# Two transformer layers on one core: exponentials left in their PSUM score bank, first layers in fewer and halved steps, a new order of the work

## The reference

```
x = layernorm(x + attn0(x))   # rms norm, global latent attention (16 heads, 4 kv heads, head size 8,
                              #   rope, q and k normed, causal), then a local one with a window of 32
x = layernorm(x + moe(x))     # 8 experts, top 2, each gelu(x @ W1 + b1) @ W2 + b2
x = layernorm(x + linear(x))  # q, k = elu(.) + 1, v; running sums over tokens, head size 64
x = layernorm(x + local(x))   # two layers: 8 heads of 64, shifted tokens, q and k of unit length,
                              #   rotary, softmax over a window of 64 plus the one before,
                              #   then a gated gelu feed-forward (341 hidden)
```

## Time and profile before

| | |
|---|---|
| median of 3 runs | 2406.52 us (2402.61 to 2421.29) |
| the profiled execution | 2405.99 us, span 2404.2 us |
| granted TensorE clock, mean | 0.916 of 2.4 GHz |
| busy: PE, PEld, DVE, ACT, POOL | 1938.3, 1187.6, 1168.7, 1166.9, 765.6 us |
| fillers (L537) | 1523 matmuls |

### The profile page before, as it was taken

The page is one execution under the profiler, slowest core; times in us unless marked ns, Lnnn a source line. Parts: engine busy times, 40 slices in busy tenths (PEclk is TensorE's granted clock), DMA queues, the critical chain, the costliest instruction groups (busy, mean ns, idle before and its releaser), DMA issues.

```text
span 2404.2 us, 40371 instructions
## 1 busy us (share of the span) xinstructions
PE 1938.3 (81%) x15498; PEld 1187.6 (49%) x15498; DVE 1168.7 (49%) x2324; ACT 1166.9 (49%) x2708; POOL 765.6 (32%) x654
## 2 busy tenths in 40 slices
PE   4885473689996899879989789859988799878886
PEld 2233371445444586534445567524445568545554
DVE  4124103655365534765346543665437543666564
ACT  2642041167853364257854265237774357236462
POOL 1420202065240523155331343026523143135350
PEclk8997596789998899989999899979999899989998
DMA  4000250000000252000000234000000044001010
GB/s 131 1 1 1 96 175 18 0 14 19 6 10 14 84 168 60 7 17 19 6 5 19 70 119 123 5 9 14 14 6 14 6 144 153 15 18 23 14 23 9
DMA packets 52945, 99.23 MB, mean 41 GB/s; under 512 B 11423, under 2 KB 26003, under 8 KB 52627
## 3 DMA queue, kind: packets, MB, share of 16 engines
q1 hardware_dynamic: 47059, 87.74, 12.3%
q0 software_dynamic: 4096, 8.40, 1.2%
q10 hardware_dynamic: 1600, 0.52, 0.1%
HBM read 66.02 MB, written 13.83 MB: 33 GB/s over the span
## 4 chain that ended last, share of the span: by engine, by line
PE 50%; DVE 21%; ACT 10%; POOL 8%; issue 7%; DMA 3%; SPq 1%; ACTq 0%; DVEq 0%; POOLq 0%
PE PB L537 4%; PE PH L778 4%; PE PD L537 4%; PE PB L1167 4%; PE PB L1187 3%; PE PB L1100 3%; PE PD L826 2%; PE PH L1011 2%; ACT front_arena L1298 2%; POOL x_rows L2118 2%; ACT back_arena L1446 2%; PE PD L1000 2%; PE PB L1121 2%; POOL front_arena L2096 2%; PE PB L1223 2%
## 5 line engine op out<-in xcount | busy, mean ns | idle before, releaser
L1298 ACT ACTIVATE front_arena<-PD 128x1024 f32<-128x1024 f32 (+3 forms) x384 | 297.0, 815 | 109.6 <-PE PD L826 107.8
L2156 POOL TENSOR_TENSOR back_arena<-back_arena 128x512 f32<-128x512 f32 x128 | 185.8, 1457 | 513.3 <-DVE back_arena L1961 513.1
L2096 POOL TENSOR_TENSOR front_arena<-front_arena,tri 128x256 f32<-128x256 f32 x256 | 190.9, 760 | 229.4 <-ACT front_arena L1298 228.3
L537 PE MATMUL PB<-ident 128*128 128x512 f16 x823 | 223.3, 392 | 23.1 <-DVE back_arena L1961 13.9
L1446 ACT ACTIVATE back_arena<-PB,fnm 128x128 f32<-128x128 f32 x512 | 181.1, 369 | 104.4 <-DVE fnm L1968 104.2
L1167 PE MATMUL PB<-wqkv,hT 128*128 128x512 f32 x384 | 216.1, 649 | 13.8 <-ACT hT L1416 9.2
L2161 POOL TENSOR_TENSOR fy<-fm,minus_half 128x16 f32<-128x16 f32 x64 | 187.5, 2930 | 77.4 <-DVE fm L1984 75.7
L1968 DVE TENSOR_REDUCE fnm<-PB 128x4 f32<-128x512 f32 x128 | 88.4, 691 | 246.5 <-PE PB L1187 246.2
L537 PE MATMUL PD<-ident 128*128 128x512 f16 x618 | 177.2, 408 | 9.9 <-DVE front_arena L1815 4.1
L778 PE MATMUL PH<-front_arena 128*32 128x512 f32 (+3 forms) x1536 | 164.9, 501 | 19.0 <-POOL front_arena L2096 17.2
L537 PEld LDWEIGHTS PB<-ident 128*128 128x128 f16 x823 | 78.3, 100 | 131.8 <-issue 41.5
(11 more groups left out here) (278 smaller groups left out, 3829.5 us busy)
## 6 DMA issues: line engine op xcount, KB each, us to landing
front_arena<-in_W SPq DMA_DIRECT2D x60, 514.0 KB, 4.9
W<-in_W SPq DMA_DIRECT2D x32, 514.0 KB, 3.6
back_arena<-back_arena SPq DMA_DIRECT2D x128, 128.0 KB, 2.4
y_rows<-front_arena SPq DMA_DIRECT2D x20, 256.0 KB, 5.5
front_arena<-x_rows SPq DMA_DIRECT2D x8, 512.0 KB, 4.2
out_y<-Nb SPq DMA_DIRECT2D x64, 32.0 KB, 1.6
X<-in_L_attn_hidden SPq DMA_DIRECT2D x56, 32.0 KB, 1.9
front_arena<-x_rows SPq DMA_DIRECT2D x4, 448.0 KB, 5.3
```

The costliest lines, as they stand in the source:

```text
L537: pe.matmul(bank[:, 0:512].rearrange("p (a b) -> p a b", b=128), ident16[:, :], ident16[:, :].unsqueeze(1).to_broadcast([128, 4, 128]), st ...
L1298: act.activation(pb[:, :, 0:n], p[:, :, 0:n], ACT.Exp, scale=INV_SQRT_HD).then_inc(freed(b, "S", half, g, kc, jp), 1)
L2096: pool.tensor_tensor(pb, pb, tri[:, :].unsqueeze(1).to_broadcast([128, 2, 128]), ALU.mult).then_inc(sg("masked"), 1)
L2156: pool.tensor_tensor(T1[k % 2][:, hs, :], T1[k % 2][:, hs, :], T2[:, hs, :], ALU.add).then_inc(sg("rot"), 1)
```

## The change

In the back, `exps` writes the exponentials over the scores in their own PSUM bank. The bank is freed by `softmax` on DVE, which reads it and writes the product to SBUF, and no longer by ACT. The exponentials wait no more until TensorE has turned the last tile's probabilities; `softmax` does. The order of the pieces in `back_labels` and the three banks are as before.

In the front: (1) the scaled x is written in two halves (`by_halves`), and its transposes, its copy and the first projections follow by halves, at every `toT`. (2) `rope` is 2 x 3 instructions over four tiles each. (3) The squares for the norm of q and k are taken by ACT from the projection's bank (into `QKsq`), before the rotation, and DVE's squaring is gone. (4) The rest of q is 2 instructions over all tiles, the first of which waits for the first of ACT's two only. (5) `rk` is 2 matmuls, and DVE does the running sum over tiles (4 small instructions more); `slots` and `sc` stand ahead of `GT` and `b2`. (6) One copy in the gate is gone. (7) `lq` and `lk` are one piece `lqk`, 128 rows high; ACT copies `lvt`; in `lo` the products that don't need the masked scores come first. (8) The sum of x into R ahead of the layer norm `x1` is moved up to the local attention's start.

Both tables are new: the fillers are 1298, in batch 0's front 114 where there were 242, in the merged batches' fronts 362 where there were 458, in batch 3's back 184 where there were 135. The diff, cut to its core:

```diff
-        for t in range(NT):
-            add(("rope", a, t), 0, 0.8, 0, 0.8)
+        for t in (0, 4):
+            add(("rope", a, t), 0, 1.7, 0, 1.7)
...
+    add(("slots",), 0, 5, 0, 5)
+    for t in range(NT):
+        add(("sc", t), 0, 3)
     add(("GT",), 1, 2.5, 1)
     add(("b2",), 2, 3, 0, 1.3)
-    add(("slots",), 0, 4, 0, 4)
-    for t in range(NT):
-        add(("sc", t), 0, 3)
...
-20003051610002030000000231111010032310000040000000000000000001002200000000000000000000000140000101000100032100510000ar00a200020170001074102230a0033060
...
+204000810000000010000000010002000220100000403000000000000000000022021000200000001010000101401000000300130501000000000000a00002010100102000112000400000
...
-                    pe.wait_ge(sg("src"), 5 * b + i + 1)
-                    for t in range(NT):
+                    pe.wait_ge(sg("src"), 10 * b + 2 * i + 1)
+                    for t in range(4):
+                        ins = pe.transpose(place(p, t), src[:, t, :], ident[:, :])
+                    ins.then_inc(sg("half_turned"), 1)
+                    pe.wait_ge(sg("src"), 10 * b + 2 * i + 2)
+                    for t in range(4, NT):
                         ins = pe.transpose(place(p, t), src[:, t, :], ident[:, :])
...
-                    for t in range(NT):
-                        pe.matmul(p[:, E * NT:E * NT + E], ones_m, both[:, E * t:E * t + E], start=(t == 0), stop=(t == NT - 1))
-                    pe.matmul(p[:, 0:NT * E], tri[:, :], both, start=True, stop=False, skip_group_check=True)
-                    for t in range(NT - 1):
-                        later = p[:, E * (t + 1):E * NT].rearrange("p (t e) -> p t e", e=E)
-                        ins = pe.matmul(later, ones_m, both[:, E * t:E * t + E].unsqueeze(1).to_broadcast([128, NT - 1 - t, E]),
-                                        start=False, stop=(t == NT - 2), skip_group_check=True)
-                    ins.then_inc(filled(b, "rk"), 1)
+                    pe.matmul(p[:, NT * E:2 * NT * E], ones_m, both, start=True, stop=True, skip_group_check=True)
+                    pe.matmul(p[:, 0:NT * E], tri[:, :], both, start=True, stop=True,
...
+                    def project(name, w, n):
                         p = fill(pe, b, name)
-                        is_free(pe, b, "toT", 3)
+                        pe.wait_ge(sg("half_xT"), 4 * b + 4)
                         for k in range(2):
-                            ins = pe.matmul(p[0:HL, 512 * k:512 * k + 512], lw[:, w, :],
+                            if k:
+                                is_free(pe, b, "toT", 3)
+                            ins = pe.matmul(p[0:HL * n, 512 * k:512 * k + 512], lw[:, w:w + n, :].rearrange("p a b -> p (a b)"),
...
                     p = fill(pe, b, "lo")
+                    is_free(pe, b, "lM")
+                    for t in range(NT):
+                        c = 128 * t
+                        pe.matmul(p[:, c + HL:c + HL + 1], lqz[:, c:c + 128], ones[0:HL, :],
+                                  start=(t % 4 == 0), stop=True, skip_group_check=True)
+                    for t in range(1, NT):
+                        c = 128 * t
+                        pe.matmul(p[:, c:c + HL], lqT[:, c:c + 128], lM[:, t, :], start=False, stop=False, skip_group_check=True)
                     pe.wait_ge(sg("l_A"), b + 1)
                     for t in range(NT):
-                        pe.matmul(p[:, 128 * t:128 * t + HL], lA[:, t, :], lkt[:, t, :],
...
-                    pe.wait_ge(sg("softmax"), 2 * k + 1 + r)
+                    is_free(pe, b, "fs", l, t, r)
...
-                    p = read(act, b, "toT", i)
-                    act.activation(xT[:, PAD:PAD + S], p, ACT.Copy).then_inc(freed(b, "toT", i), 1)
+                    act.wait_ge(sg("half_turned"), 4 * b + i + 1)
+                    p = slot(b, "toT", i)
+                    act.activation(xT[:, PAD:PAD + 512], p[:, 0:512], ACT.Copy).then_inc(sg("half_xT"), 1)
+                    read(act, b, "toT", i)
+                    act.activation(xT[:, PAD + 512:PAD + S], p[:, 512:S], ACT.Copy).then_inc(freed(b, "toT", i), 1)
...
-                                act.activation(QK[:, 4 * i:4 * i + 4, :], p[:, :, 0:160], ACT.Copy).then_inc(freed(b, "qkv", a, i), 1)
+                                act.activation(QK[:, 4 * i:4 * i + 4, :], p[:, :, 0:160], ACT.Copy).then_inc(sg("qk_in"), 1)
+                                act.activation(QKsq[:, 4 * i:4 * i + 4, :], p[:, :, 0:160], ACT.Square).then_inc(freed(b, "qkv", a, i), 1)
...
                     if k:
-                        read(act, *of_tile("fp", k - 1, r))
+                        act.wait_ge(sg("inverted"), 2 * k - 1 + r)
                     for h in range(4 * r, 4 * r + 4):
                         c = 128 * (h - 4 * r)
-                        ins = act.activation(fP[:, h, :], p[:, c:c + 128], ACT.Exp,
+                        ins = act.activation(p[:, c:c + 128], p[:, c:c + 128], ACT.Exp,
                                              bias=fnm[:, h:h + 1], accum_out=fden[:, h:h + 1])
-                    ins.then_inc(freed(b, "fs", l, t, r), 1)
...
+                def by_halves(dst, src):
+
+                    for h in range(2):
+                        hs = slice(4 * h, 4 * h + 4)
+                        dve.tensor_tensor(dst[:, hs, :], src[:, hs, :], st_y[:, hs].unsqueeze(2).to_broadcast([128, 4, D]),
+                                          ALU.mult).then_inc(sg("src"), 1)
+                    counts["src"] = counts.get("src", 0) + 2
+                    dve.wait_ge(sg("src"), counts["src"])
 
...
-                    for t in range(NT):
-                        yield front_at(b, "rope", a, t)
-                        if t % 4 == 0:
-                            is_free(dve, b, "qkv", a, t // 4)
-                        dve.tensor_tensor(rv[:, t], qv[:, t],
-                                          rope[a][:, t, 0:1, :].to_broadcast([128, nh, HD]), ALU.mult)
+                    for i in range(2):
+                        yield front_at(b, "rope", a, 4 * i)
+                        dve.wait_ge(sg("qk_in"), 4 * b + 2 * a + i + 1)
+                        ts = slice(4 * i, 4 * i + 4)
+                        dve.tensor_tensor(rv[:, ts], qv[:, ts],
+                                          rope[a][:, ts, 0, :].unsqueeze(2).to_broadcast([128, 4, nh, HD]), ALU.mult)
                         for s in range(2):
-                            ins = dve.tensor_tensor(tmp[:, t, :, :, s], sw[:, t, :, :, 1 - s],
-                                                    rope[a][:, t, 1:2, :].rearrange("p o (d s) -> p o d s", s=2)[:, :, :, s].to_broadcast([128, nh, HD // 2]), ALU.mult)
+                            turn = rope[a][:, ts, 1, :].rearrange("p t (d s) -> p t d s", s=2)[:, :, :, s]
+                            ins = dve.tensor_tensor(tmp[:, ts, :, :, s], sw[:, ts, :, :, 1 - s],
...
-                    link(dve.tensor_tensor(arena_rope, QR, QR, ALU.mult))
...
-                    dve.wait_ge(sg("q_hi"), 4 * b + 2 * a + 2)
-                    qv4 = QR[:, :, 0:128].rearrange("p t (j g d) -> p t j g d", j=GQ, g=KV)
+                    qv4 = QR[:, :, 0:128].rearrange("p t (n d) -> p t n d", d=HD)
+                    qs4 = Qs.rearrange("p t j g s d -> p t (j g) s d")
                     for s in (2, 3):
-                        for t in range(NT):
-                            ins = dve.tensor_tensor(Qs[:, t, :, :, s, :], qv4[:, t], Qs[:, t, :, :, s - 2, :], ALU.subtract)
+                        dve.wait_ge(sg("q_hi"), 4 * b + 2 * a + s - 1)
+                        ins = dve.tensor_tensor(qs4[:, :, :, s, :], qv4, qs4[:, :, :, s - 2, :], ALU.subtract)
                     signals(ins, "split")
...
+                    if a == 1:
+                        yield front_at(b, "S1", 0, 0)
+                        link(dve.tensor_tensor(R[:, :, :], R[:, :, :], XX[b % 2][:, :, :], ALU.add))
...
+                    link(dve.tensor_copy(one_tile, each))
+                    link(dve.tensor_tensor_scan(flat(upto), flat(runs), flat(one_tile), 0.0, ALU.mult, ALU.add))
+                    dve.tensor_tensor(ahead, upto.rearrange("p e t -> p t e"), one_tile.rearrange("p e t -> p t e"), ALU.subtract)
...
+                    yield front_at(b, "b2")
+                    p = read(dve, b, "b2").rearrange("p (t n) -> p t n", t=NT)
+                    frees(dve.tensor_tensor(R[:, :, :], XX[b % 2][:, :, :], p, ALU.add), b, "b2")
...
+                    pqk = read(dve, b, "lqk")
+                    signals(dve.tensor_scalar(lm[0], pqk, 0.0, None, ALU.min), "l_min")
...
-                    is_free(dve, b, "fs", l, t, r)
+                    k = (b * DEPTH + l) * NT + t
+                    dve.wait_ge(sg("exps"), 2 * k + 1 + r)
                     ws = slice(4 * r, 4 * r + 4)
                     dve.reciprocal(frd[:, ws], fden[:, ws]).then_inc(sg("inverted"), 1)
 
                 def softmax(b, l, t, r):
                     k = (b * DEPTH + l) * NT + t
```

(7 more changed lines are left out.)

133 lines of the change are left out of this document (66 added, 67 removed), and 16 rows, old and new, of the table RUNS.

## The result

The changed kernel takes 2511.39 us (median of 4 runs, 2505.42 to 2518.7) against 2407.29 us: a ratio of 1.042, interval 1.037 to 1.048. The forecast was 2366 with a range up to 2436. How much a stage differs between traces, unchanged code shows: the first stage of the changed kernel takes 403.6 to 409.3 us in six traces, and its first merged stage 596 us on the comparison chip and 608 on that of run 4.

A forecast was written before the change was run, and what follows sets the result against it. First stage bound by latency, merged stages close to bound by PE, the last in between. 2406 - 48 (batch 0's front) - 24 (merged stages, net) + 32 (hold, last stage) = 2366 us, range 2312 to 2436.

The forecast's parts named there:

- front's edits, first stage: Batch 0's front, where nothing covers it: set-up, routing, gate, linear attention and fillers save 48 us, bounds 36 and 60.
- front's edits, three merged stages: Merged stages: set-up 8, routing about 7, x1 1, linear attention and fillers 5, together 21 us saved a stage.
- hold, merged stages: Merged stages: the longer-held bank costs 2.65 us in about 5 of 12 tile steps, 13 us a stage.
- hold, last stage: Last stage: `k` and the keys' turn wait for the product, 2.65 us in each of 12 steps, +32 us.
- the price of the bank held longer: Back's tile steps: 2.65 us more per paying step, +32 us in the last stage and 13 in each merged one.
- the first rival: Merged stages: the hold is paid in every step, 32 us against a gain of 16; 2438 us, slower; 17%.
- the upper bound of 45: Last stage's hold: up to 45 us, since PE idles over 4 of 13 us and its clock may fall.
- 12.2 + 1.2 + 3: Batch 0's front: attention set-up and rest of q save 12.2 us, moved x sum about 1.2, other fillers 3.
- 11.7 + 3 us: Batch 0: 38 of 60 linear-attention fillers removed save 11.7 us, other fillers, as before the second attention, 3.
- the third rival: First stage: with 242 fillers cut to 114 the clock falls and takes back 20 us; 2386, no change; 18%.
- PSUM operands: Back: exponentials written to PSUM and the product reading PSUM (0.69 against 0.68 us) were each taken as 0.
- The fourth rival: Back: ACT gains by writing PSUM, 24 ns for each exponential; 2354 us; 5%.

The follow-up runs named there:

- comparison chip: Another chip of the same kind, where the kernel before took 2474 us and the changed kernel 2572 us, ratio 1.039.
- run 4: Changed kernel with the last stage's scores in the two idle PD banks, exponentials still in PSUM: 2516.37 us, ratio 1.015 to the kernel before.
- run 1: Changed kernel with exponentials and product in SBUF and the score bank freed by the exponentials: 2438.75 us, ratio 0.984 to the kernel before.
- run 7: Kernel before with the front's edits alone, old order and fillers, exponentials in SBUF: 2405.26 us, ratio 0.971.
- run 5: Changed kernel with more fillers in the last stage, written to a PD bank while TensorE waits: 2567.04 us, beside the changed kernel's 2571.95.
- run 8: Changed kernel with exponentials in SBUF and the old filler count at each label: 2451.91 us, ratio 0.988 to the kernel before.
- run 10: Front's edits alone, old order and fillers, no hold, product 0 ahead of the queries' rotary on VectorE: 2353.26 us, ratio 0.975 to the kernel before.
- run 2: Kernel before with only the exponentials kept in PSUM until the product, product 1 issued one piece earlier: 2702.95 us, ratio 1.090.
- run 3: Kernel before with the hold alone: all in SBUF, score bank freed by the product, product 1 issued one piece earlier: 2704.2 us, ratio 1.091.

## Why the prediction was wrong

Spans of traces on three chips, on which the kernel before has nearly the same time (2474, 2477 and 2481 us), give the account. As the chips differ, a stage is good to some 10 us and a term of the whole to some 15: by the ratios, each on its own chip, the hold costs 136 us and the order 33.

| term | forecast | measured |
|---|---|---|
| front's edits, first stage | -48 | -36 |
| front's edits, three merged stages | -63 | -37 |
| hold, merged stages | +39 | +82 |
| hold, last stage | +32 | +51 |
| new order and fillers without the hold (run 1 less run 7) | within the front's terms | +38 |
| difference of run 1 in the first stage, same instructions | | -5 |
| sum | -40 | +93 |

**The step that failed is the price of the bank held longer.** It was forecast at 71 us and is 133 in the stages with a back. That is 62 of the 133 us between forecast and result; the front's gain, 38 short, and the new order, for which the sum had no term, at 38, make up the rest. Three things were wrong in the price.

*How many steps pay.* I let 5 of 12 steps of a merged stage pay, because in the others pieces of the front stand between `s` 0 and `k`. They don't always cover the wait, since VectorE has the front's own passes ahead of the product too. In the merged stages TensorE waits for the product 53 times, 115 us in all; with the exponentials in SBUF it is 5 times, 4 us:

```profile
PE PB L1175 <- DVE back_arena L2028: 52.1, 19, 7.1
PE PB L1212 <- DVE back_arena L2028: 27.7, 8, 6.4
PE PB L540 <- DVE back_arena L2028: 20.1, 12, 2.7
PE PB L1222 <- DVE back_arena L2028: 12.1, 11, 2.2
...
```

(Waits of TensorE in these three stages of the changed kernel on the comparison chip: total, times, longest.) The longest is 7.1 us, not 2.65. `s` 1 ended at 1983.13 there, and VectorE was busy with the front's layer norm before it came to the scores (same trace, timeline of DVE; `k` starts at 1990.21):

```profile
1980.77 1.22 DVE L1618 TENSOR_REDUCE st_a<-N 128x8 f32<-128x1024 f32 x1
...
1984.03 1.29 DVE L1602 TENSOR_TENSOR X<-X,st_y 128x512 f32<-128x512 f32 x2 [1.83 <-POOL st_y L2104]
1985.35 0.69 DVE L1997 TENSOR_REDUCE fnm<-PB 128x4 f32<-128x512 f32 x1
...
1989.47 0.68 DVE L2028 TENSOR_TENSOR back_arena<-PB,frd 128x512 f32<-128x512 f32 x1
```

This was the first rival, with 17%. It came true in mechanism and sign: 27 us a stage against its 32. Its 2438 fell short of the result because it kept the front's full gain, had nothing for the new order and took 32 in the last stage.

*What an extra piece does.* For the last stage I gave 20 us as the lower bound "since steps 2, 3 and 7 have another piece between". It is the reverse. In a ring of three an extra piece moves a later piece on to a held bank: `o` comes to wait 4.0 us for product 1, three times in that stage (12.2 us). With TensorE kept warm (run 5) the six bare steps cost 2.9 us more on average and the six others 3.9, the dearest 6.8. The step of the earlier trace rows itself was forecast rightly, by its parts (`k` at 6.03 us, 13.0 to 13.5 us long). I multiplied the best step by twelve.

*The clock.* The last stage ran at 0.89 on the comparison chip and at 0.87 on the first, where the kernel before had 0.96 and 0.95. It costs some 8 us of 49, by run 5. I had it in the upper bound of 45 only.

**The front's gain was right in mechanism, too large in size.** Halves, rotation, rest of q and scatters came out about as worked out. In the first stage the marks show -9.2 us up to the first layer norm (forecast 12.2 + 1.2 + 3 = 16.4), -15.5 from there to the second (13 + 1.8 = 14.8) and -12.3 to the third (16).

The fillers that were taken out are the term that failed here. The forecast gave 11.7 + 3 us for them. Runs 7, 8 and 10 have the front's edits with the old fillers: their first stages take 404.4, 412.6 and 412.1 us, those with the new fillers 403.6 to 409.3 in six traces. On average that is a gain of 3 us, not 14.7. It is less than the spread of single traces, but its shortfall is as much as 11 of the 12 us that are missing. What the fewer fillers save, the clock takes back. The stretch from the scale to the reduction in the local attention's set-up shows it, windows of the changed kernel and of run 8:

```profile
160.93:171.74 10.81, 9.97 (x98) 8.21 (x98) 5.95 (x9) 3.79 (x6) 0.00 (x0) 0.72 0.01 2
161.20:170.35 9.15, 8.41 (x101) 5.92 (x99) 5.96 (x10) 3.69 (x6) 0.00 (x0) 1.00 0.01 2
```

With the old fillers in front the clock is 1.00, the projections take 1.34 us and the stretch the 9.1 us of the forecast; with the new ones the clock is 0.72, they take 2.41 us and the stretch 1.7 more. That is the third rival's mechanism (18%), at a little over half its price of 20. In the merged stages the front's 21 became 12; where the missing 9 go, no run separates.

**The new order** was taken as part of the terms. With its fillers it is a term of its own, and perhaps with both signs: it costs 38 us where there is no hold, while the hold costs 54 us a merged stage in the old order (run 2) and 27 in the new. The second half isn't shown alone, as run 2 has the old front too.

**PSUM operands.** The 0 taken for them was right: runs 2 and 3 are equal. By the Trainium skill's table, which has a higher fixed cost from PSUM (VectorE: DVE Perf Modes, The TRN2 errata), the product would have become dearer. It became cheaper, 683 ns for 735 on average:

```profile
L2028 DVE TENSOR_TENSOR back_arena<-PB,frd 128x512 f32<-128x512 f32 x128 | 87.5, 683 | 1.9 <-DVE front_arena L1746 0.6
```

Undisturbed, the two places cost the same; the average fell because a product from SBUF is slower beside POOL's multiplications and additions. In the kernel before, 88 of the 128 products start beside no POOL instruction and take 685 ns; 13 start while POOL multiplies or adds in SBUF (L2096, L2156) and take 943 and 1433 ns on average. In the changed kernel those that start so take 682 and 686.

The fourth rival had the right size and no effect: an exponential takes 344 ns where it took 369, 25 less, and runs 2 and 3 show no time saved by it.

## What to carry to other kernels

A bank that is kept longer must be priced by everyone who comes to it in turn: write out the ring for each kind of step, the odd ones with an extra piece above all, and price the wait from the last reader's end, with all that stands ahead of that reader on its engine. Whether the pieces between cover the wait depends on the engine that is waited for, not on the one that waits. And if a hold must be, put the release first on its engine (55 us here for one moved call) or give the held tiles banks of their own (53 us in one stage); an order made for one set of waits should be made anew, or put back, when the waits go. And a filler on the chain is not a gain of its own length when it goes: here 136 of them were worth some 3 us.

## What the runs showed that I had not expected

- POOL's addition of the rotary (128x512, both inputs in SBUF) takes 1278 ns on average in the changed kernel and 1457 before. It comes with the product reading PSUM in place of SBUF: in the last stage of run 3, 24 of the 32 additions have over 0.5 us of the product beside them and take 1.62 to 1.66 us, the other 8 take 1.26 to 1.28; in run 2, with the same waits, as many have the product beside them and all 32 take 1.26 to 1.28. It lies off the path. One addition with the product beside it, run 3, then run 2:

```profile
2566.46 1.65 POOL L2157 TENSOR_TENSOR back_arena<-back_arena 128x512 f32<-128x512 f32 x1 [4.90 <-DVE back_arena L1961]
2570.16 1.27 POOL L2160 TENSOR_TENSOR back_arena<-back_arena 128x512 f32<-128x512 f32 x1 [5.37 <-DVE back_arena L1961]
```

- The kernel before takes 2407 to 2481 us from chip to chip. Its first and last stages are equal on two of them (440.6 and 440.0, 289.6 and 286.9); the merged stages are 558, 567 and 549 on one and 584, 577 and 584 on the other, at a granted clock of 0.93 to 0.94 and of 0.90 to 0.94. The clock is not all of it: of the 72 us more in the merged stages TensorE is busy for 33 and idle for 39. The ratio of the change hardly moves with it (1.042 and 1.039).
